# Attention sums: VectorE's first addition reads two neighbouring tiles instead of copying one, and key tiles and couples of maxima move

## The reference, cut to what matters

```python
q = _split_heads(x @ Wq + bq, h)
k = _split_heads(x @ Wk + bk, h)
v = _split_heads(x @ Wv + bv, h)
pattern = jnp.einsum('bhid,bhjd->bhij', k, q) * scale
prob = jax.nn.softmax(pattern, axis=-2)
out = jnp.einsum('bhis,bhid->bhsd', prob, v)
```

## Time and profile before

| | us |
|---|---|
| median of 3 runs | 4653.44 |
| lowest and highest | 4646.86, 4657.02 |
| the profiled execution | 4646.07 |
| its span | 4644.1 |
| PE busy | 4351.6 (94%) |
| DVE busy | 3295.5 (71%) |
| POOL busy | 2707.8 (58%) |
| ACT busy | 2175.5 (47%) |

### The profile page before, as it was taken

How to read it: one execution, slowest core, us unless ns; L and a number is a source line. 1 busy time by engine, 2 the same in 40 slices (tenths; PEclk the granted TensorE clock), 3 DMA queues, 4 the chain that set the end, 5 groups by cost and what they waited for, 6 DMA issues and landing times.

```text
span 4644.1 us, 67290 instructions
## 1 busy us (share of the span) xinstructions
PE 4351.6 (94%) x25496; PEld 2560.7 (55%) x25496; DVE 3295.5 (71%) x4434; ACT 2175.5 (47%) x3523; POOL 2707.8 (58%) x1205
## 2 busy tenths in 40 slices
PE   7999999999999999999999999858999897999898
PEld 5445454554554545545545545426777665777665
DVE  6777877777777777777787787476666455666455
ACT  5445444444444444444444444315666443666442
POOL 2867767667666676676676776804454332454332
PEclk8999999999999999999999999979999998999999
DMA  2000000000000000000000000010000100000001
GB/s 79 6 11 13 8 11 5 16 11 6 11 15 6 11 6 16 11 5 11 15 6 11 13 8 7 1 59 1 1 1 0 38 1 19 1 1 1 1 1 37
DMA packets 81401, 55.73 MB, mean 12 GB/s; under 512 B 48532, under 2 KB 71016, under 8 KB 81128
## 3 DMA queue, kind: packets, MB, share of 16 engines
q1 hardware_dynamic: 81128, 51.92, 4.2%
HBM read 30.66 MB, written 4.19 MB: 8 GB/s over the span
## 4 chain that ended last, share of the span: by engine, by line
PE 44%; POOL 25%; issue 12%; DVE 11%; ACT 7%; POOLq 1%; DMA 1%; SPq 0%; DVEq 0%; ACTq 0%
POOL accp L770 21%; PE psum L1521 8%; PE psum L1533 8%; PE psum L1668 5%; PE psum L1488 4%; PE psum L1798 2%; PE psum L1714 2%; PE psum L1728 2%; ACT lp L967 2%; POOL accp L766 2%; PE psum L1811 2%; DVE accd L1176 2%; PE psum L1465 2%; PE psum L1705 2%; PE psum L1473 1%
## 5 line engine op out<-in xcount | busy, mean ns | idle before, releaser
L770 POOL TENSOR_TENSOR accp<-accp,prob 128x1024 f32<-128x1024 f32 x704 | 1768.6, 2512 | 492.2 <-ACT prob L921 414.2
L921 ACT ACTIVATE prob<-psum 128x1024 f32<-128x1024 f32 x1024 | 1020.5, 1025 | 1462.7 <-PE psum L1521 1374.6
L1153 DVE TENSOR_REDUCE mx<-psum 128x1 f32<-128x512 f32 x1984 | 1277.2, 685 | 347.3 <-PE psum L1488 298.8
L1533 PE MATMUL psum<-prob,vv 128*64 128x512 f32 x4096 | 992.9, 606 | 0.0
L1488 PE MATMUL psum<-kh,qh 64*128 64x512 f32 x2048 | 492.2, 470 | 56.7 <-DVE mx L1153 48.6
L1533 PEld LDWEIGHTS psum<-prob,vv 128*64 128x64 f32 x4096 | 248.6, 136 | 490.1 <-issue 420.4
L787 POOL TENSOR_TENSOR lp<-lp,lrcp 128x1024 f32<-128x1024 f32 x128 | 242.6, 1895 | 451.7 <-DVE lrcp L1293 451.7
L1488 PEld LDWEIGHTS psum<-kh,qh 64*128 64x128 f32 x2048 | 205.0, 184 | 522.9 <-DVE mx L1153 442.2
L1521 PE MATMUL psum<-nm,one 64*128 64x512 f32 x2048 | 429.1, 408 | 14.1 <-ACT prob L921 6.5
L1521 PE MATMUL psum<-qh,kh 64*128 64x512 f32 x2048 | 412.3, 391 | 0.0
L1521 PE MATMUL psum<-qh,kl 64*128 64x512 f32 x2048 | 412.0, 391 | 0.0
(11 more groups left out here) (197 smaller groups left out, 6797.3 us busy)
## 6 DMA issues: line engine op xcount, KB each, us to landing
kl<-kl SPq DMA_DIRECT2D x64, 256.0 KB, 3.8
wqk<-L_attn_Wq SPq DMA_DIRECT2D x64, 64.0 KB, 2.1
rot_l<-const_rot SPq DMA_DIRECT2D x2, 2048.0 KB, 9.0
out<-lpT SPq DMA_DIRECT2D x32, 128.0 KB, 1.7
wqkv_l<-L_ffn_wqkv SPq DMA_DIRECT2D x4, 768.0 KB, 10.4
w_l<-L_ffn_w SPq DMA_DIRECT2D x4, 618.0 KB
wqk<-L_attn_Wk SPq DMA_DIRECT2D x32, 64.0 KB, 2.0
wv_p<-L_attn_Wv SPq DMA_DIRECT2D x16, 128.0 KB, 2.3
```

The lines of the kernel that those rows point to most:

```text
L770: pool.tensor_tensor(acc_p[cp][:], first[:], prob[kt % PRING][:], ALU.add).then_inc(pool_sum, 1)
L921: act.activation(prob[t % PRING][:], psum[:, S_BANK + 2 * (t % 2):S_BANK + 2 * (t % 2) + 2, :].rearrange("p a b -> p (a b)"), ACT.Exp, sca ...
L1153: dve.tensor_reduce(mx4[:, e, qt, c:c + 1], ps, AX_X, ALU.max).then_inc(ring_free, 1)
L1533: mm = pe.matmul(psum[j * DH:(j + 1) * DH, O_BANK, :], vv[:, kt, s * DH:(s + 1) * DH], prob[t % PRING][:, j * T:(j + 1) * T], start=(kt == ...
```

## The change

DVE's tiles now differ between the halves: (8, 9, 12) in the first, (2, 3, 10) in the second. The first instruction adds the first two tiles, the second adds the third, so that DVE has two additions in a half and no copy; POOL keeps thirteen tiles and JOIN. In `max_places` the weights of the two groups behind the middle sum change from 0 and 2 to 2 and 3.

```diff
-SUM_DVE = (3, 7, 11)
-SUM_POOL = tuple(k for k in range(KT) if k not in SUM_DVE)
+SUM_DVE = ((8, 9, 12), (2, 3, 10))
+SUM_POOL = tuple(tuple(k for k in range(KT) if k not in tiles) for tiles in SUM_DVE)
...
-            weight[SUM0_GROUP + 1:SUM0_GROUP + 3] = [0, 2]
+            weight[SUM0_GROUP + 1:SUM0_GROUP + 3] = [2, 3]
...
+        def dve_used(cp, kt):
+
+            return max(SUM_DVE[cp].index(kt), 1)
...
-                kt = SUM_DVE[j]
-                dve.wait_ge(exp_done, G * STEPS + cp * KT + kt + 1)
-                if j:
-                    dve.wait_ge(dve_sum, G * (CP * DVE_OPS) + OFF_DVE + cp * DVE_OPS + j)
-                    dve.tensor_tensor(acc_d[cp][:], acc_d[cp][:], prob[kt % PRING][:], ALU.add).then_inc(dve_sum, 1)
-                else:
-                    dve.tensor_copy(acc_d[cp][:], prob[kt % PRING][:]).then_inc(dve_sum, 1)
+                tiles = SUM_DVE[cp]
+                dve.wait_ge(exp_done, G * STEPS + cp * KT + tiles[j] + 1)
+                left = prob[tiles[0] % PRING]
+                if j > 1:
+                    dve.wait_ge(dve_sum, G * (CP * DVE_OPS) + OFF_DVE + cp * DVE_OPS + j - 1)
+                    left = acc_d[cp]
+                dve.tensor_tensor(acc_d[cp][:], left[:], prob[tiles[j] % PRING][:], ALU.add).then_inc(dve_sum, 1)
```

More of the change, by code:

```diff
@@ L38 @@
 PRING = 4
-SUM_DVE = (3, 7, 11)
-SUM_POOL = tuple(k for k in range(KT) if k not in SUM_DVE)
+SUM_DVE = ((8, 9, 12), (2, 3, 10))
+SUM_POOL = tuple(tuple(k for k in range(KT) if k not in tiles) for tiles in SUM_DVE)
 JOIN = -1
-POOL_SEQ = SUM_POOL[1:-1] + (JOIN,) + SUM_POOL[-1:]
-POOL_OPS = len(POOL_SEQ)
-DVE_OPS = len(SUM_DVE)
+POOL_SEQ = tuple(tiles[1:-1] + (JOIN,) + tiles[-1:] for tiles in SUM_POOL)
+POOL_OPS = len(POOL_SEQ[0])
+DVE_OPS = len(SUM_DVE[0]) - 1
 QK_ITEMS, V_ITEMS = CHUNKS, 4
@@ L407, in adaln_block, with pool_used @@
         OFF_S, OFF_POOL, OFF_DVE, OFF_RING = STEPS, CP * POOL_OPS, CP * DVE_OPS, RING_PAIR
-        def pool_used(kt):
-            return 1 if kt == SUM_POOL[0] else POOL_SEQ.index(kt) + 1
+        def pool_used(cp, kt):
+            return 1 if kt == SUM_POOL[cp][0] else POOL_SEQ[cp].index(kt) + 1
+        def dve_used(cp, kt):
+            return max(SUM_DVE[cp].index(kt), 1)
         def phase_end(eng, phase):
@@ L760, in head_sums @@
                 for cp in range(CP):
-                    for i, kt in enumerate(POOL_SEQ):
+                    for i, kt in enumerate(POOL_SEQ[cp]):
                         n = G * (CP * POOL_OPS) + OFF_POOL + cp * POOL_OPS + i
@@ L768, in head_sums @@
                         pool.wait_ge(exp_done, G * STEPS + cp * KT + kt + 1)
-                        first = acc_p[cp] if i else prob[SUM_POOL[0] % PRING]
+                        first = acc_p[cp] if i else prob[SUM_POOL[cp][0] % PRING]
                         pool.tensor_tensor(acc_p[cp][:], first[:], prob[kt % PRING][:], ALU.add).then_inc(pool_sum, 1)
@@ L916, in exps @@
                     cp, kt = divmod(t - PRING, KT)
-                    if kt in SUM_DVE:
-                        act.wait_ge(dve_sum, G * (CP * DVE_OPS) + OFF_DVE + cp * DVE_OPS + SUM_DVE.index(kt) + 1)
+                    if kt in SUM_DVE[cp % CP]:
+                        act.wait_ge(dve_sum, G * (CP * DVE_OPS) + OFF_DVE + cp * DVE_OPS + dve_used(cp % CP, kt))
                     else:
-                        act.wait_ge(pool_sum, G * (CP * POOL_OPS) + OFF_POOL + cp * POOL_OPS + pool_used(kt))
+                        act.wait_ge(pool_sum, G * (CP * POOL_OPS) + OFF_POOL + cp * POOL_OPS + pool_used(cp % CP, kt))
                     act.activation(prob[t % PRING][:], psum[:, S_BANK + 2 * (t % 2):S_BANK + 2 * (t % 2) + 2, :].rearrange("p a b -> p (a b)"),
@@ L1213, in pair @@
                             cp, kt = divmod(j, KT)
-                            if kt in SUM_DVE:
-                                add_sum(G, cp, SUM_DVE.index(kt))
+                            if kt in SUM_DVE[cp][1:]:
+                                add_sum(G, cp, SUM_DVE[cp].index(kt))
                         elif kind == "sum":
```

## The result

The changed kernel takes 4669.2 us (median of 8 runs, 4662.68 to 4673.47), the kernel before 4651.88 in the same comparison (8 runs, 4644.69 to 4657.02): 1.0039 of the time before, with a 95% interval of 1.003 to 1.0048, so slower by about 17 us. The profiled execution took 4669.73 us with a span of 4667.8. Forecast were 4666, with a sum of +12.4 us.

The account below looks back on a forecast made before the run. PE, busy 94% of the span, was taken as the bound. Even heads −18.2, odd heads +29.6 and the last head +1 gave +12.4 us: 4658.5 on the profiled execution, 4666 as a median, range 4644 to 4691.

Parts of the forecast that it names:

- The price of a third couple: Groups of three against two: a third couple costs 0.68 us; six such groups become four, −1.36 us a head.
- Behind the middle sum: Groups 11 and 12: opening couple 5.88 us after the sum, a stall of 1.7; +1.04 us a head.
- The odd heads' additions: Behind groups 6, 9, 13: end 1.62 into the next group, stalling groups 7 and 10 by 0.99; odd heads +1.85 us.
- The even heads: Copy and addition stalls go (−1.79), one behind group 4 comes (+0.81); −1.30 us a head in all.
- group 14: Odd heads' group of two behind an addition: second couple at 2.37 instead of 2.18, +0.19 us.
- The bridge: Keeps its couples, loses the copy's stall, gets one ahead of group 10: about 0.
- The last head: Without couples, POOL's third tile of the second half waits for the first addition, then an exponential: about +1 us.
- A: Odd heads' additions at ends of groups 6, 9, 13 meet a free POOL: faster, −20 us, 4633; chance 0.12.
- B: PE's clock falls in the new stall, in half of 30 heads: +25 us, 4691; chance 0.13.
- C: Odd heads: only one of the two 0.99 stalls appears, or both at 0.35; 4649 to 4655; chance 0.2.
- D: The change doesn't do what it says; only its effect was called open, covered in A and C.

Follow-up runs that it names:

- no opening couple: Changed kernel with one couple instead of two in group 12, the other moved to another group: 4634.09 us, 0.9955 of the kernel before.
- both: Changed kernel with one couple in group 12 and the odd heads' groups of three ahead of groups of two: 4590.41 us, 0.9869 of before.
- Threes moved: Changed kernel with the odd heads' groups of three couples moved to groups 4, 6, 9 and 13: 4629.01 us, 0.9949 of before.
- GpSimd waits: Changed kernel with GpSimd's tile 14 (first half) and 4 (second) held until DVE's addition is done: 4633.56 us, 0.9971 of before.
- tiles only: Kernel before with DVE's new tiles, couples placed as before: 4655.21 us, 1.0012 of before.
- a longer stall: Changed kernel with one more, unused DVE reduction inside each head's middle normalising: 4706.25 us, 1.0125 of before.

## Why the prediction was right, step by step

- **The price of a third couple.** 0.68 us, taken from two groups, held: moving such groups in *no opening couple* and *both* gave the head times worked out from it.
- **Behind the middle sum.** 5.88 us from the sum to the opening couple were forecast from the bridge's rows, and 5.88 were measured. That its stall is an order's and not a load's was shown by *no opening couple*.
- **The odd heads' additions.** This was the one price without a row of its own, bounded between none and 2.3 us a stall. Forecast were an end 1.62 into the next group and a stall of 0.99; measured are 1.63 and 1.00. *Threes moved* and *GpSimd waits* removed the stalls in two independent ways, with gains of 40 and 31 us, so both parts of the cause are shown: the phase of GpSimd, and a middle couple that needs DVE early.
- **The even heads.** Gone are the stalls of copy and additions, and the new one behind group 4 came at 2.98, forecast 2.99.
- **Sizes that were off.** The sum was 12.4; 17 were measured between the medians, and 18 in the heads of the two traces. Odd heads cost 2.06 and not 1.85: group 14 gave 0.31 and not 0.19. Its second couple came at 2.38 as forecast, 0.20 late, but the values started 0.42 behind the start of that couple, which had waited, where 0.32 is normal. Groups of two ran at 4.38 and not 4.36. Even heads gained 1.18 and not 1.30: the interval that holds group 5's stall was 5.30, 0.93 above one without, and not 0.81, with the same 0.1 behind the couple that waited. The last pair's even head, counted among the fourteen, gained only 0.14, because the low clock at its end lasted longer. The bridge cost 0.7 where I had put nothing, above all in its group behind the fourth output tiles (+1.0), which I had not worked out. The last head cost nothing where I had put 1. So four terms were too low by 6.7 us in all and one too high by 1.1, and 12.4 + 5.6 gives the 18; the mechanisms, and not a cancelling of errors, gave the number.
- **Rivals.** A (an idle GpSimd, faster) did not come by itself: in the changed kernel 127 of the 128 additions end 1.1 us behind the end of a GpSimd addition. B (the clock) did not come in the new stall, but one longer by 0.6 to 0.7 brings it in 13 of 30 heads, and in *tiles only* it came behind 1.57 us of idle time at another place, so its staying away was not assured by the stall's length alone. C fell: both stalls came at full size, 1.00, in each odd head. (Its times were mis-added: −7 to −3 us on the median of 4653 is 4646 to 4650, and not 4649 and more. The forecast doesn't hang on it.) D fell.

Not tried: a different pair of tiles for DVE in odd and even heads, and other splits of tiles between DVE and GpSimd.

## What to carry to other kernels

Where one engine is bound and runs in a written order, a helper's load says little; ask at which time into each of its groups the helper gives back the buffer that the group needs next, and place long operations of the helper where the next need comes late. When DVE and GpSimd both add in SBUF, the later one waits for the earlier one's operation to end, so the phase between them, and even an added wait that puts the short and urgent one first, can be worth more than the operations removed. And when two edits free an engine in one place and load it in another, run each alone: here one was +3 us, the other +74, and together +17, while the same work in a better order gives −57, and −73 with one added wait.

## What the runs showed of the hardware that I had not expected

An idle time of PE of 1.67 us left its granted clock at 1.00 in 30 of 30 heads of the changed kernel. One of 2.38 us brought it to 0.50 in 11 of 15 odd heads of *a longer stall*, one of 2.25 in 2 of 15 others, and one of 1.57 in 3 of 14 even heads of *tiles only*. So the length of the idle time alone does not decide: a shorter one can bring the fall at one place where a longer one does not at another, and equal ones in the same place bring it in some heads and not in others. In the attention of all these kernels each fall stands behind an idle time of PE, the shortest of 1.56 us. What else decides was not tried. "TensorE: Matmul & The Clock Gate", "What's actually happening", of the Trainium skill has the clock follow how busy PE has recently been; the runs agree in that each fall came behind an idle time. A fall behind these stalls cost 1.2 to 1.6 us a head.

DVE's addition ends 1.1 us behind the end of the GpSimd addition that it met, in 127 of the 128 cases in either kernel, and takes 1.22 when it meets none. It holds the other way round too. DVE's addition at 1881.52, shown above, has 0.93 us left when GpSimd's next one begins:

```profile
1882.01 3.18 POOL L774 TENSOR_TENSOR accp<-accp,prob 128x1024 f32<-128x1024 f32 x1 [0.16 <-POOL accp L774]
```

It takes 3.18 us where 2.37 is normal, and ends 2.25 behind the end of DVE's.
